# First weight chunk in float32, last chunk bank by bank, shift sums 1 to 3 inside the turns of a cross-attention kernel

## The reference, cut to what matters

```python
q = jnp.einsum('bte,ef->btf', emb, Wq) + bq
k = jnp.einsum('bml,le->bme', latent, Wk) + bk
v = jnp.einsum('bml,le->bme', latent, Wv) + bv
w = jnp.einsum('bte,bme->btm', q, k) * scale
w = jax.nn.softmax(w, axis=1)
pred = jnp.einsum('btm,bme->bte', w, v)
x = pred + emb
return (x - mu) * jax.lax.rsqrt(var + EPS) * gamma + beta
```

## Time and profile before

| | |
|---|---|
| median of 3 runs | 144.66 us (144.46 to 144.82) |
| the profiled execution | 144.95 us, span 143.2 us |
| PE busy | 134.4 us, 94% of the span |
| DVE busy | 117.3 us, 82% |
| ACT busy | 81.6 us, 57% |
| POOL busy | 65.2 us, 46% |

### The profile page before, as it was taken

How to read it: one execution, slowest core, us unless ns; L and a number is a source line. 1 busy time by engine, 2 the same in 40 slices (tenths; PEclk the granted TensorE clock), 3 DMA queues, 4 the chain that set the end, 5 groups by cost and what they waited for, 6 DMA issues and landing times.

```text
span 143.2 us, 2969 instructions
## 1 busy us (share of the span) xinstructions
PE 134.4 (94%) x1046; PEld 129.4 (90%) x1046; DVE 117.3 (82%) x216; ACT 81.6 (57%) x286; POOL 65.2 (46%) x61
## 2 busy tenths in 40 slices
PE   6998999999899999999999999999999999999910
PEld 6998999999898999999999999999999999998900
DVE  0689989999777899759999975899699976876992
ACT  4677349459527836385564729475665628483520
POOL 1000000009031594735758472666667463659891
PEclk9999999999999999999999999999999999999996
DMA  4999999965057597897896889699897886545113
GB/s 141 300 406 421 421 300 395 317 213 194 5 205 237 195 307 243 328 346 259 314 311 259 322 256 402 215 316 326 252 306 250 331 273 225 217 146 178 73 73 146
DMA packets 10670, 37.33 MB, mean 261 GB/s; under 512 B 1184, under 2 KB 1184, under 8 KB 10656
## 3 DMA queue, kind: packets, MB, share of 16 engines
q1 hardware_dynamic: 9424, 34.92, 69.5%
q10 hardware_dynamic: 1232, 2.23, 4.1%
HBM read 33.87 MB, written 3.28 MB: 259 GB/s over the span
## 4 chain that ended last, share of the span: by engine, by line
PE 75%; DVE 10%; DMA 4%; POOL 3%; issue 2%; ACT 2%; SPq 1%; POOLq 1%
PE ps_U L400 28%; PE ps_S L386 27%; PE ps_Y L421 12%; DMA xT_in<-xT 4%; DVE xT_lo L647 3%; PE ps_U L361 3%; DVE xu L659 2%; PE ps_Y L361 2%; POOL xT_in L848 2%; PE ps_w L409 1%; SPq L255 1%; DVE wkq L637 1%; DVE W_lo L744 1%; POOL xT_in L836 1%; POOL rstd L841 1%
## 5 line engine op out<-in xcount | busy, mean ns | idle before, releaser
L521 ACT ACTIVATE expo<-scores,negmax 121x100 f32<-121x100 f32 x96 | 35.0, 366 | 27.3 <-DVE negmax L679 27.3
L386 PE MATMUL ps_S<-G,ctxT_in 128*121 128x100 f32 (+1 forms) x384 | 43.5, 270 | 0.0
L400 PEld LDWEIGHTS ps_U<-prob,ctx_in 121*128 121x128 f32 x360 | 42.1, 192 | 0.9
L400 PE MATMUL ps_U<-prob,ctx_in 121*128 121x100 f32 x360 | 42.5, 274 | 0.0
L386 PEld LDWEIGHTS ps_S<-G,ctxT_in 128*121 128x121 f32 (+1 forms) x384 | 42.0, 185 | 0.0
L825 POOL TENSOR_TENSOR prob<-expo,rinv 121x600 f32<-121x600 f32 x16 | 19.0, 1189 | 35.7 <-DVE rinv L686 35.7
L841 POOL TENSOR_TENSOR rstd<-vareps,neg_half 128x1 f32<-128x1 f32 (+1 forms) x13 | 12.4, 955 | 22.8 <-DVE vareps L717 22.5
L836 POOL TENSOR_TENSOR xT_in<-x_in,xT_in 128x512 f32<-128x512 f32 (+1 forms) x13 | 16.6, 1276 | 13.0 <-issue 8.4
L690 DVE TENSOR_REDUCE probsum<-prob 121x100 f32<-121x600 f32 x16 | 19.8, 1239 | 3.0 <-POOL prob L825 2.7
L521 ACT ACTIVATION_READ_ACCUMULATOR expo<-scores,negmax 121x1 f32 x96 | 18.0, 187 | 0.0
L675 DVE TENSOR_TENSOR scores<-ps_S,c_rows 121x600 f32<-121x600 f32 x16 | 12.5, 782 | 5.8 <-PE ps_S L386 5.6
(11 more groups left out here) (91 smaller groups left out, 175.8 us busy)
## 6 DMA issues: line engine op xcount, KB each, us to landing
ctx_in<-ctx SPq DMA_DIRECT2D x16, 768.0 KB, 5.7
ctxT_in<-ctxT SPq DMA_DIRECT2D x16, 722.0 KB, 5.2
xT_in<-xT SPq DMA_DIRECT2D x8, 400.0 KB, 8.8
x_in<-x SPq DMA_DIRECT2D x12, 256.0 KB, 4.7
out<-xT_in ACTq DMA_DIRECT2D x8, 256.0 KB, 4.2
wqk<-Wqk SPq DMA_DIRECT2D x4, 388.0 KB, 4.3
out<-xT_in SPq DMA_DIRECT2D x3, 256.0 KB, 2.0
wv_in<-Wv SPq DMA_DIRECT2D x1, 512.0 KB, 16.1
```

The lines of the kernel that those rows point to most:

```text
L386: last = nc.tensor.matmul(ps_scores(c)[0:rows(c), :], ctxT_in[:, q, l * M + c * MP:l * M + c * MP + rows(c)], G[:, l, bass.ds(b * T, T)], ...
L400: last = nc.tensor.matmul(ps_U[:, q, l * T:(l + 1) * T], ctx_in[0:rows(c), q, c, l * P:(l + 1) * P], prob[0:rows(c), q, c * T:(c + 1) * T] ...
L521: last = nc.scalar.activation(expo[0:MP, q, c * T:(c + 1) * T], scores[0:MP, q, c * T:(c + 1) * T], ACT.Exp, bias=negmax[0:MP, q, c:c + 1] ...
```

## The change

1. WARM is 8 instead of 9. Chunk 0 of the weights is no longer split: four float32 matmuls on the input tiles themselves take the place of its 12 float32r ones. Its upper and lower parts on ACT and DVE go, and wk_hi is made on DVE for chunks 1 to 3.
2. In the last chunk the hi x hi products still run over the four banks; then each bank gets its last two products together, so that the banks become complete one after the other.
3. Group 0's second half of xT_hi is copied on DVE instead of ACT. project(g) waits for each half of xT_hi and xT_lo where it first uses it. The bias sums move into project(1), behind its first 8 matmuls.
4. The shift sums of groups 1 to 3 move back: sum_shift(1) behind project(3), sum_shift(2) behind turn 4, sum_shift(3) behind turn 7, and the steps of ACT and DVE that feed them move with them. result takes the last 512 columns of xT_in's groups 0 and 1 instead of group 2.

The core of the diff:

```diff
+
+            pe.wait_ge(w_in[0], 16)
+            for e in range(EC):
+                nc.tensor.matmul(banks[e][:, 0:L + 2], wqT[:, 0, e * P:(e + 1) * P], wkT[:, 0, :], start=True, stop=False)
+            for f in range(1, EC):
+                pe.wait_ge(wkhi_set, f)
+                pe.wait_ge(wqhi_set, f)
                 for e in range(EC):
-                    nc.tensor.matmul(banks[e][:, 0:L + 2], wq_hi[:, f, e * P:(e + 1) * P], wk_hi[:, f, :],
-                                     start=(f == 0), stop=False)
...
+                if f < EC - 1:
+                    pe.wait_ge(wklo_set, f)
+                    for e in range(EC):
...
+            pe.wait_ge(wklo_set, EC - 1)
+            pe.wait_ge(wqlo_set, EC - 1)
+            for e in range(EC):
+                nc.tensor.matmul(banks[e][:, 0:L + 2], wq_hi[:, EC - 1, e * P:(e + 1) * P], wk_lo[:, EC - 2, :],
+                                 start=False, stop=False)
+                nc.tensor.matmul(banks[e][:, 0:L + 2], wq_lo[:, EC - 1, e * P:(e + 1) * P], wk_hi[:, EC - 2, :],
+                                 start=False, stop=True).then_inc(W_summed, 1)
...
+                            pe.wait_ge(xTlo_set, 2 * g + e // EH + 1)
+                        if n < EC and e % EH == 0:
+                            wait_upper_x(pe, g, e // EH)
...
+                    if g == 1 and n == EC:
+                        bias_sums()
...
-                                        start=True, stop=True)
-            last.then_inc(gbias_summed, 1)
             project(1)
             scores_of(0, 0)
             sum_shift(0)
             project(2)
             scores_of(1, 1)
+            project(3)
             sum_shift(1)
-            project(3)
-            sum_shift(2)
             turn(2, 0)
-            sum_shift(3)
             pe.wait_ge(Wvhi_set, 1)
             pe.wait_ge(Wvlo_set, 1)
-            each_turn(turn, 3)
+            turn(3, 1)
+            turn(4, 0)
+            sum_shift(2)
+            turn(5, 1)
+            turn(6, 0)
+            turn(7, 1)
+            sum_shift(3)
...
-                for h in range(2):
+                for h in range(1 if g == 0 else 2):
...
             take_group(0)
+            upper_half(2)
             upper_shift(0)
-            upper_half(2)
             take_group(1)
             upper_half(3)
-            upper_shift(1)
             take_shift(0)
             exponentials(0, 0)
             take_group(2)
-            upper_shift(2)
+            upper_shift(1)
             act.wait_ge(wv_loaded, 16)
             nc.scalar.activation(Wv_hi[:, :, :], wv_in[:, :, :], ACT.Copy).then_inc(Wvhi_set, 1)
-            take_shift(1)
             exponentials(1, 1)
             take_group(3)
-            take_shift(2)
-            upper_shift(3)
+            take_shift(1)
             act.wait_ge(rows_in, 48)
             upper_U(0, 0)
             exponentials(2, 0)
-            take_shift(3)
+            upper_shift(2)
             value_bias(0)
             exponentials(3, 1)
-            each_turn(turn, 4)
+            turn(4, 0)
+            turn(5, 1)
+            take_shift(2)
+            upper_shift(3)
+            turn(6, 0)
+            turn(7, 1)
+            turn(8, 0)
+            take_shift(3)
+            each_turn(turn, 9)
...
+            dve.wait_ge(xT_loaded[0][1], 16)
+            nc.vector.tensor_copy(xT_hi[:, 0, EH:, :], xT_in[:, 0, EH:, :]).then_inc(first_xThi_set, 1)
             lower_half(0)
...
             weigh_by_u(0)
+            lower_half(2, (0,))
             lower_shift(0)
-            weigh_by_u(1)
-            lower_half(2)
+            lower_half(2, (1,))
             dve.wait_ge(mask_set, 2)
             dve.wait_ge(scores_zeroed, 1)
             maxima(0, 0)
-            lower_shift(1)
             lower_half(3)
-            weigh_by_u(2)
+            weigh_by_u(1)
             normaliser(0, 0)
             maxima(1, 1)
+            lower_shift(1)
             chunk_sum(0, 0)
-            lower_shift(2)
-            weigh_by_u(3)
             dve.wait_ge(rows_in, 48)
-            lower_shift(3)
             normaliser(1, 1)
             maxima(2, 0)
             lower_U(0, 0)
+            weigh_by_u(2)
             chunk_sum(1, 1)
             normaliser(2, 0)
             maxima(3, 1)
+            lower_shift(2)
             add_residual(0)
             row_stats(0)
             chunk_sum(2, 0)
             centre(0)
-            each_turn(turn, 4)
+            turn(4, 0)
+            weigh_by_u(3)
+            turn(5, 1)
+            turn(6, 0)
+            lower_shift(3)
+            each_turn(turn, 7)
             normaliser(B - 1, 1)
             lower_U(B - 3, 1)
             lower_U(B - 2, 0)
```

More of the change, by code:

```diff
@@ L129, in xattn @@
         wqhi_set = sem("wqhi_set")
-        first_wkhi_set = sem("first_wkhi_set")
         wkhi_set = sem("wkhi_set")
@@ L145, in xattn @@
         mask_set = sem("mask_set")
+        first_xThi_set = sem("first_xThi_set")
         xThi_set = sem("xThi_set")
@@ L193, in xattn @@
         resid = spare[:, 1, 0:2 * E].rearrange("p (q e) -> p q e", e=E)
-        result = spare[:, 2, 0:2 * E].rearrange("p (q e) -> p q e", e=E)
+        result = spare[:, 0:2, 2 * E:3 * E]
         y = wv_in
@@ L241, in exists, with wait_upper_x @@
             return 0 <= b < B
-        def wait_upper_wk(engine, c):
-            if c == 0:
-                engine.wait_ge(first_wkhi_set, 1)
+        def wait_upper_x(engine, g, h):
+            if g == 0 and h == 1:
+                engine.wait_ge(first_xThi_set, 1)
             else:
-                engine.wait_ge(wkhi_set, c)
+                engine.wait_ge(xThi_set, 2 * g + h + (1 if g == 0 else 0))
         block = stack.enter_context(nc.Block())
@@ new lines, in _, with bias_sums @@
+            pe.wait_ge(wklo_set, EC - 1)
+            pe.wait_ge(wqlo_set, EC - 1)
+            for e in range(EC):
+                nc.tensor.matmul(banks[e][:, 0:L + 2], wq_hi[:, EC - 1, e * P:(e + 1) * P], wk_lo[:, EC - 2, :],
+                                 start=False, stop=False)
+                nc.tensor.matmul(banks[e][:, 0:L + 2], wq_lo[:, EC - 1, e * P:(e + 1) * P], wk_hi[:, EC - 2, :],
+                                 start=False, stop=True).then_inc(W_summed, 1)
+            def bias_sums():
+                pe.wait_ge(wkq_step, EC)
+                for c in range(LC):
+                    last = nc.tensor.matmul(ps_w[:, c:c + 1], wkq[:, (EC - 1) % 2, c * P:(c + 1) * P], ones[:, 0:1],
+                                            start=True, stop=True)
+                last.then_inc(gbias_summed, 1)
@@ L438, in _ @@
             project(0)
-            pe.wait_ge(wkq_step, EC)
-            for c in range(LC):
-                last = nc.tensor.matmul(ps_w[:, c:c + 1], wkq[:, (EC - 1) % 2, c * P:(c + 1) * P], ones[:, 0:1],
-                                        start=True, stop=True)
-            last.then_inc(gbias_summed, 1)
             project(1)
@@ L568, in _ @@
             nc.scalar.activation(ones_r[:, :], ones[:, :], ACT.Copy).then_inc(onesr_set, 1)
-            for f in range(EC):
+            for f in range(1, EC):
                 act.wait_ge(w_in[f], 16)
-                if f > 0:
-                    nc.scalar.activation(wk_hi[:, f, :], wkT[:, f, :], ACT.Copy).then_inc(wkhi_set, 1)
                 nc.scalar.activation(wq_hi[:, f, :], wqT[:, f, :], ACT.Copy).then_inc(wqhi_set, 1)
@@ L621, in _ @@
             nc.vector.memset(neg_half[:, :], -0.5).then_inc(consts_set, 1)
-            for c in range(EC):
+            for c in range(1, EC):
                 dve.wait_ge(w_in[c], 16)
[L624 to L629, removed]
+                nc.vector.tensor_copy(wk_hi[:, c - 1, :], wkT[:, c, :]).then_inc(wkhi_set, 1)
+                dve.wait_ge(wkhi_set, c)
+                nc.vector.tensor_tensor(wk_lo[:, c - 1, :], wkT[:, c, :], wk_hi[:, c - 1, :].bitcast(F32),
+                                        ALU.subtract).then_inc(wklo_set, 1)
+                dve.wait_ge(wqhi_set, c)
+                nc.vector.tensor_tensor(wq_lo[:, c, :], wqT[:, c, :], wq_hi[:, c, :].bitcast(F32),
+                                        ALU.subtract).then_inc(wqlo_set, 1)
             def weigh_by_bq():
@@ L644, in lower_half @@
                     dve.wait_ge(G_summed, g - 1)
-                for h in range(2):
-                    dve.wait_ge(xThi_set, 2 * g + h + 1)
+                for h in parts:
+                    wait_upper_x(dve, g, h)
                     nc.vector.tensor_tensor(xT_lo[:, q, h * EH:(h + 1) * EH, :], xT_in[:, g, h * EH:(h + 1) * EH, :],
```

30 lines of the change are left out of this document (11 added, 19 removed).

## The result

The changed kernel took 148.71 us (median), the kernel before 144.75 in the same comparison: a ratio of 1.0266, 95% interval 1.0246 to 1.0287. It is 2.7% slower; the forecast was 148.1 us. The profiled execution took 148.63 us (span 146.9), 3.68 us more than that of before. One of the changed kernel's six executions (151.17 us) and one of e8_short_finish's four (150.48 us) were in a slower state that some executions fall into; the medians count them, the ratios leave them out.

A forecast was written before the change was run, and what follows sets the result against it. PE's own work bounds the turns, and DVE's room there decides the sign: tile 2's values 2.99 us later plus shift sum 3's 0.44 make 3.43 us on 144.66, so 148.1 us; forecast range 147.4 to 149.0 us (0.50).

The forecast's parts named there:

- DVE's chain: From lower_U(0) to the maxima of batch 5: 20.93 us busy plus 0.6 held by POOL, ending 2.54 us later.
- PE's lead: At the end of the first weighted_ctx, PE 1.1 us earlier than in the kernel before.
- ACT's two steps: take_shift(2) and upper_shift(3) ahead of upper_U(3), behind exponentials(5): 1.03 us more delay for lower_U(3).
- The first chunk: Head: four float32 matmuls take 1.9 us instead of 1.47; one warm-up less saves 0.41; second chunk at 6.3.
- At nothing: Net cost given to the float32 first chunk in the head, with -0.9 and +1.4 as ends.
- Bank by bank: Last weight chunk: first projection 0.66 us earlier, near 10.7; DVE's lower halves 0.8 late; 0.35 us survives.
- The projections: Waits of 0.2 and 0.41 us and a 0.44 us shift sum go; a 0.3 us wait comes.
- The wait of 0.3 us for lower_shift(1): In the projections, lower_shift(1) meets POOL computing Wv_lo, so PE waits 0.3 us (0 to 1.0).
- rival (4): In the turns, POOL's port lock catches weigh_by_u(3), or rinv(2) behind residual(0): 149.0 to 150.0 us, chance 0.13.
- PE's idle time: 4.1 us, about half ahead of the values of tile 1, the rest ahead of scores(6) and tile 2's values.
- Rival (5): PE's clock falls in the new idle time; half the level costs some 3 us, 151 us; chance 0.04.
- Rivals (1) and (2): Turns: (1) DVE has room, about 144.0 us, chance 0.07; (2) stalls just eat the lead, 144.3 to 145.1, 0.04.

The follow-up runs named there:

- e8_short_finish: The changed kernel with POOL's finish(1) cut to one column; 147.98 us, ratio 1.0207 to the kernel before.
- e5_both_moved: The changed kernel with weigh_by_u(2), lower_shift(2) ahead of lower_U(0), weigh_by_u(3) in turn 9, group 3's shift steps in turn 10, ACT's take_shift(2) later; 143.91 us, ratio 0.9927.
- e9_split_chunk: e5_both_moved with weight chunk 0 split again into 12 float32r matmuls and 9 warm-up matmuls; 143.85 us, ratio 0.9926 to the kernel before.
- e4_wbu2_early: The changed kernel with weigh_by_u(2) and lower_shift(2) ahead of lower_U(0), and ACT's upper_shift(2) ahead of upper_U(0); 146.52 us, ratio 1.0130.
- e3_act_later: The changed kernel with ACT's take_shift(2) and upper_shift(3) behind upper_U(3) and value_bias(2); 148.38 us, ratio 1.0238 to the kernel before.
- e7_filled: The changed kernel with nine float32 matmuls of constants filling PE's wait ahead of the values of tile 1; 148.82 us, ratio 1.0274.
- e6_wbu3_turn9: The changed kernel with weigh_by_u(3) moved into turn 9 and upper_shift(3), sum_shift(3), take_shift(3) to turn 10; 147.05 us, ratio 1.0140.
- e2_shift_only: The kernel before with only the shift sums, their ACT and DVE steps and the place of result changed; 149.46 us, ratio 1.0306.

## Why the prediction was right, and where it was not

The time was right, the sign was right, and the mechanism was: DVE's chain from lower_U(0) to the maxima of batch 5 is over full, and PE waits for it in two pieces. e5_both_moved is the proof by the opposite: take 5 us of work out of that stretch and nothing is lost. But that the sum, 3.43 us, came within 0.25 of the 3.68 measured is luck in part. PE's lead was 0.8 us larger than forecast, the DVE chain 1.26 us longer, ACT's two steps 0.2 us cheaper, and -0.8 + 1.26 - 0.2 is about the 0.25 that is left.

**The first chunk.** 1.9 us taken, with the second chunk at 6.3. In the profiled execution it took 6.23 - 4.68 = 1.55 us, but it began at 4.68 and not at 4.42: between these two traces a warm-up matmul less was worth 0.15 us, not 0.41. The two errors nearly cancel. "At nothing" was right to within 0.7 us, by e9_split_chunk.

**Bank by bank.** The first projection began at 10.89 instead of 11.36, forecast 10.7. The copy of 800 columns took 0.58 us, not 0.75, and W_lo came at 12.34 instead of 11.89: 0.45 us late, not 0.8. PE kept all of its 0.47 us (scores of batch 0 at 20.17 instead of 20.64), not 0.35.

**The projections.** The wait of 0.3 us for lower_shift(1) did not come. The step was held, as the prediction said, and longer (2.50 us), but it ended at 34.25, before PE came from project(3) to shift sum 1 at 34.37. I had priced the hold and not asked where PE would be by then. The lead on the kernel before is 0.47 us at scores of batch 0, 0.96 at those of batch 1 (27.46, before 28.42) and 1.91 at those of batch 2. So the 0.2 us wait gave back 0.49 (its row counts from the modelled end of a matmul, and the pace of the stream was lost with it), and shift sum 2 with its wait 0.95 instead of 0.85. Lead 1.91 us, not 1.1: an error of 0.8 us that made the forecast too slow.

**DVE's chain.** 20.93 + 0.6 = 21.53 us forecast, 22.79 measured. lower_shift(2) beside POOL's probabilities took 1.45 us: 0.9 more than a free one, not 0.6. The other 0.9 is rival (4): weigh_by_u(3), 2.87 us instead of 1.98, held by finish(1) (e8_short_finish). I gave it 0.13 because no row of before showed such a step beside POOL. It happened in the other place with a POOL step beside it too: 2.78 in e4_wbu2_early. So rival (4)'s condition came true, and its time, 149.0 to 150.0, did not, because the larger lead paid for it.

**ACT's steps.** 1.03 us forecast, 0.8 in the trace of e3_act_later.

**PE's idle time.** 4.1 us forecast, 1.85 + 1.35 = 3.2 measured. PE had 0.8 us more of lead to lose, so the gap should have been larger. The missing part went into the slow clock: 5.66 - 4.14 = 1.5 us of longer matmuls in the same gap.

**Rival (5)** named that mechanism, and I argued it away by a stretch at the end of the kernel where no matmul ran and the clock column stayed at 1.00. That argument failed: here 1.85 us of idle time were followed by 0.50. Its price, 3 us, was wrong as well: the slow matmuls took 1.5 us longer, and none of it reached the time (e7_filled), for a reason that I had not written down. A slow PE costs nothing while DVE is later. Where DVE is not later, the fall is paid for: the slower executions of e6_wbu3_turn9 fit that.

**Rivals (1) and (2)**, with room on DVE, needed the two weigh_by_u to fit ahead of lower_U(1) and lower_U(3). They didn't; DVE never waited between 40.61 and 64.5 us.

## What to carry to other kernels

Before moving work off one engine's waits, find where the engine that does the work has room: here the same 5 us of DVE work, with one pair of ACT's steps, cost 4.8 us of time in the full turns (148.71 against 143.91) and nothing in DVE's idle time ahead of them and in a turn without an output tile. A step that stands behind another engine's SBUF work costs nothing if its reader arrives later anyway, so price a hold by the time at which its reader comes. And a gap on PE that is closed at only one place can move to the next: in e4_wbu2_early the 1.9 us ahead of the values of tile 1 went, and the wait behind them grew from 1.4 to 2.5 us (0.7 + 1.8).

## What the runs showed of the hardware

**The clock after a short idle time is not the same in every execution.** After 1.85 us of idle time ahead of the same matmuls, the granted clock fell to 0.50 in the traces of the changed kernel, of e2_shift_only and of e8_short_finish, and stayed at 1.00 in those of e3_act_later and e6_wbu3_turn9. The mean clocks of executions without a trace fit: 0.980 to 0.983 in all six of the changed kernel, 0.993 to 0.995 in the four of e7_filled, where the idle time is filled. What decides it stays open.

**TensorE's pace at the start differs too.** The pieces of the first chunk in bank ps_S, matmul durations in ns (min/median/max), of the changed kernel and then of e5_both_moved:

```profile
L329 PE MATMUL ps_S<-wqk x4: 381/381/383, 4.7 to 5.3; 128*128 128x258 f32 x4
```

```profile
L329 PE MATMUL ps_S<-wqk x4: 636/638/639, 4.7 to 6.0; 128*128 128x258 f32 x4
```

The same instructions behind the same warm-up took 381 ns in one trace and 638 in the other, though the granted clock's column stood at 1.00 from the first microsecond in both. The chunk then took 1.55 us or 2.6. The traced execution of e5_both_moved was the slowest of its four (144.33 us; the others 143.00 to 144.11), which fits, but the others have no trace.

**DVE's steps on two SBUF tensors were held by POOL's wide steps; beside its one-column step no hold shows.** xu_lo took 0.57 us alone and 1.06 to 2.50 beside a POOL step of 600 or 1024 columns, the three steps of weigh_by_u 1.98 alone and 2.78 to 2.87 beside one of 512 or 600. In the changed kernel xu_lo once began inside POOL's inverse_deviation, which works on one column, and took its free 0.57 us:

```profile
72.12 0.99 POOL L871 TENSOR_TENSOR rstd<-vareps,neg_half 128x1 f32<-128x1 f32 x1 [2.00 <-DVE vareps L741]
```

```profile
72.61 0.57 DVE L690 TENSOR_TENSOR xu_lo<-xu,xu_hi 128x400 fp32r<-128x400 f32 x1
```

Whether such a step holds DVE for a shorter time or not at all stays open; POOL's spans are rough.
